# Maxima of two query tiles in one vector instruction, and the value products in one run, in the first attention of a two-layer transformer kernel

## The reference

```python
c_q = x @ Wq_down
c_kv = x @ Wkv_down
q_c = (c_q @ Wq_up).reshape(b, s, N_HEADS, HEAD_DIM)
q_r = (x @ Wq_rope).reshape(b, s, N_HEADS, ROPE)
k_c = (c_kv @ Wk_up).reshape(b, s, N_HEADS, HEAD_DIM)
v_c = (c_kv @ Wv_up).reshape(b, s, N_HEADS, HEAD_DIM)
k_r = x @ Wk_rope
scores = (jnp.einsum('bqhd,bkhd->bhqk', q_c, k_c) + jnp.einsum('bqhd,bkd->bhqk', q_r, k_r)) / scale
attn = jax.nn.softmax(scores, axis=-1)
out = jnp.einsum('bhqk,bkhd->bqhd', attn, v_c)
```

## Time and profile before

| | |
|---|---|
| median of 3 runs | 2729.01 us (2726.97 to 2730.4) |
| profiled execution, from its first to its last instruction | 2727.7 us |
| granted TensorE clock, mean | 0.976 of full speed |
| first attention's loop, first to last row of line 407 | 62.9 to 1499.9 us |
| busy: TensorE, DVE, ACT | 94%, 58%, 41% of the span |

### The profile page before, as it was taken

One profiled execution on the slowest core, in us unless ns is written; L12 is line 12 of the kernel. 1 busy time (PEld: TensorE's weight loads), 2 busy tenths in 40 slices (PEclk: granted clock), 3 DMA queues, 4 the chain that ended last, 5 costly groups with the idle time before them and its releaser, 6 DMA issues. The chain is left out here.

```text
span 2727.7 us, 38579 instructions
## 1 busy us (share of the span) xinstructions
PE 2571.7 (94%) x12487; PEld 1838.7 (67%) x12487; DVE 1579.8 (58%) x2919; ACT 1129.2 (41%) x1832; POOL 439.7 (16%) x519
## 2 busy tenths in 40 slices
PE   6999999999999999999999759989999999999996
PEld 3666666666666666666666436658778778778774
DVE  5666666666666666666666260137566566566566
ACT  3455555555555555555555230014234234243231
POOL 0101010101010101010100010004343343242320
PEclk8899999999999999999999969989999999999998
DMA  5122121212121212121211240010110110110001
GB/s 190 44 43 49 41 49 41 49 41 49 41 49 41 49 41 49 41 49 41 49 41 41 69 138 0 0 54 24 39 38 0 38 38 0 38 38 0 16 1 51
DMA packets 46693, 116.86 MB, mean 43 GB/s; under 512 B 5313, under 2 KB 22721, under 8 KB 40514
## 3 DMA queue, kind: packets, MB, share of 16 engines
q1 hardware_dynamic: 46658, 116.40, 16.3%
HBM read 71.81 MB, written 10.49 MB: 30 GB/s over the span
## 5 line engine op out<-in xcount | busy, mean ns | idle before, releaser
L407 DVE TENSOR_REDUCE row_max<-ps_max 128x1 f32<-128x512 f32 x1024 | 678.1, 689 | 294.0 <-PE ps_max L472 270.4
L361 ACT ACTIVATE probs<-ps_score 128x1024 f32<-128x1024 f32 x512 | 525.6, 1027 | 123.8 <-PE ps_score L487 92.5
L472 PE MATMUL ps_max<-KX,Q 68*128 68x512 f32 x1024 | 396.3, 418 | 46.0 <-DMA KX<-content_k 41.2
L485 PE MATMUL ps_score<-Q,K 128*128 128x512 f32 x1024 | 409.1, 400 | 0.5 <-ACT probs L361 0.5
L487 PE MATMUL ps_score<-Q,K 97*128 97x512 f32 x1024 | 405.7, 396 | 0.0
L472 PEld LDWEIGHTS ps_max<-KX,Q 68*128 68x128 f32 x1024 | 194.3, 190 | 207.1 <-issue 150.3
L401 DVE TENSOR_TENSOR Q<-ps_x,Q 64x512 fp32r<-64x512 f32 x256 | 176.5, 690 | 240.7 <-ACT Q L356 238.9
L356 ACT ACTIVATE Q<-ps_x 64x512 fp32r<-64x512 f32 x256 | 151.9, 593 | 365.3 <-PE ps_x L457 363.8
L497 PE MATMUL ps_o<-probs,V_slot 128*32 128x512 f32 x2048 | 245.8, 598 | 1.1 <-ACT probs L361 1.1
L485 PEld LDWEIGHTS ps_score<-Q,K 128*128 128x128 f32 x1024 | 194.2, 190 | 54.9 <-ACT probs L361 12.1
L487 PEld LDWEIGHTS ps_score<-Q,K 97*128 97x128 f32 x1024 | 194.8, 190 | 41.0
(11 more groups left out here) (217 smaller groups left out, 3952.8 us busy)
## 6 DMA issues: line engine op xcount, KB each, us to landing
Q<-Q SPq DMA_DIRECT2D x64, 512.0 KB, 4.3
w_raw<-in_w_qrope SPq DMA_DIRECT2D x32, 512.0 KB, 3.7
wq_raw<-in_wq SPq DMA_DIRECT2D x8, 1024.0 KB, 5.6
wo_raw<-in_wo SPq DMA_DIRECT2D x8, 1024.0 KB, 4.9
w_raw<-in_w SPq DMA_DIRECT2D x6, 704.0 KB, 4.1
Q<-content_q SPq DMA_DIRECT2D x64, 64.0 KB
K<-content_k SPq DMA_DIRECT2D x64, 64.0 KB
wkv_raw<-in_wkv SPq DMA_DIRECT2D x8, 512.0 KB, 3.5
```

Source lines behind the costliest of these rows:

```text
L361: act.activation(probs[:, j, 2 * half:2 * half + 2, :], ps_score[half][:, :, :], ACT.Exp, scale=SCALE).then_inc(exped, 1)
L407: dve.tensor_reduce(row_max[:, t, j:j + 1], ps_max[t % 2][:, :], axis=AXX, op=ALU.max)\
L472: pe.matmul(ps_max[t % 2][:, :], Q2[0:KC0, b, j, t * P:(t + 1) * P], KX[0:KC0, b, j, :], start=True, stop=True).then_inc(max_made, 1)
L485: pe.matmul(ps_score[half][:, k, :], K1[:, b, t * P:(t + 1) * P], Q1[:, b, j, :], start=True, stop=False)
```

## The change

The two single banks for maxima become one double bank `ps_max` of 128 x 2 x 512. The matmuls of two query tiles (2 half and 2 half + 1) are issued together into its two banks, and one DVE instruction reduces both, over the innermost axis, into two columns of `row_max`. So a step has 8 entries `m` instead of 16. A pair waits until the reduction of the pair before it is done. In `ORDER` all four value products come first, ahead of the first maximum, and the eight pairs are spread over the rest. The turned maxima go to the first bank of the pair.

```diff
-        ps_max = [own.enter_context(nc.psum_tensor(f"ps_max{i}", [P, S], F32)) for i in range(2)]
+        ps_max = own.enter_context(nc.psum_tensor("ps_max", [P, 2, S], F32))
...
-            "v00 v10 m00 v20 v30 m01 q00 m02 q10 m03 m10 q20 m11 s00 l00 m12 s01 m13 "
-            "s10 o00 m20 s11 m21 s20 m22 m23 s21 m30 s30 m31 m32 s31 m33").split()]
+            "v00 v10 v20 v30 m00 q00 m01 q10 m10 q20 m11 s00 l00 s01 "
+            "s10 o00 m20 s11 m21 s20 m30 s21 s30 m31 s31").split()]
...
-            def take_max(n, j, t):
-                dve.wait_ge(max_made, 16 * n + 4 * j + t + 1)
-                dve.tensor_reduce(row_max[:, t, j:j + 1], ps_max[t % 2][:, :], axis=AXX, op=ALU.max)\
+            def take_max(n, j, half):
+                dve.wait_ge(max_made, 8 * n + 2 * j + half + 1)
+                dve.tensor_reduce(row_max[:, 2 * half:2 * half + 2, j], ps_max[:, :, :], axis=AXX, op=ALU.max)\
                    .then_inc(max_taken, 1)
...
-            def max_scores(g, b, n, j, t, wait_free=True):
-
-                if j % 2 == 0 and t == 0:
+            def max_scores(g, b, n, j, half, wait_free=True):
+
+                if j % 2 == 0 and half == 0:
                     pe.wait_ge(q_high, 2 * n + j // 2 + 1)
-                if j == 0 and t == 0:
+                if j == 0 and half == 0:
                     pe.wait_ge(content_in[b], 80 * (g + 1))
                     if wait_free:
                         pe.wait_ge(row_made, n)
                 if wait_free:
-                    pe.wait_ge(max_taken, 16 * n + 4 * j + t - 1)
-                pe.matmul(ps_max[t % 2][:, :], Q2[0:KC0, b, j, t * P:(t + 1) * P], KX[0:KC0, b, j, :],
-                          start=True, stop=True).then_inc(max_made, 1)
+                    pe.wait_ge(max_taken, 8 * n + 2 * j + half)
+                for k in range(2):
+                    t = 2 * half + k
+                    last = pe.matmul(ps_max[:, k, :], Q2[0:KC0, b, j, t * P:(t + 1) * P], KX[0:KC0, b, j, :],
+                                     start=True, stop=True)
+                last.then_inc(max_made, 1)
...
-                    pe.wait_ge(max_taken, 16 * (n + 1))
+                    pe.wait_ge(max_taken, 8 * (n + 1))
```

More of the change, by code:

```diff
@@ L383, in body @@
                         act.wait_ge(row_in, 16 * n)
-                    act.activation(mrow[0:GH, :], ps_max[0][0:GH, :], ACT.Copy, scale=-1.0).then_inc(row_made, 1)
+                    act.activation(mrow[0:GH, :], ps_max[0:GH, 0, :], ACT.Copy, scale=-1.0).then_inc(row_made, 1)
                     if not (first and b == 0):
@@ L427, in _ @@
                 for j in range(2 * pair, 2 * pair + 2):
-                    for t in range(ST):
-                        take_max(0, j, t)
+                    for half in range(2):
+                        take_max(0, j, half)
             def body(g, first, last):
@@ L513, in _ @@
             for j in range(GH):
-                for t in range(ST):
-                    max_scores(0, 0, 0, j, t, wait_free=4 * j + t >= 2)
+                for half in range(2):
+                    max_scores(0, 0, 0, j, half, wait_free=j + half > 0)
             def body(g, first, last):
@@ L528, in body @@
                             queries(g + b, 1 - b, 0, third)
-                    pe.wait_ge(max_taken, 16 * (n + 1))
+                    pe.wait_ge(max_taken, 8 * (n + 1))
                     for t in range(ST):
-                        ins = pe.transpose(ps_max[0][0:GH, t * P:(t + 1) * P], row_max[:, t, :], ident[:, :])
+                        ins = pe.transpose(ps_max[0:GH, 0, t * P:(t + 1) * P], row_max[:, t, :], ident[:, :])
                     ins.then_inc(max_turned, 1)
```

## The result

The changed kernel took 2935.09 us (median of 4 runs, 2927.59 to 2938.82) against 2727.99 us for the kernel before in the same session: ratio 1.0755, 95% interval 1.0735 to 1.0774. It is 7.5% slower. The profiled execution is the fastest of the four (2927.59 us); its span is 2925.8 us, 198.1 us more than before.

The account below looks back on a forecast made before the run. TensorE, busy 94%, bounds the kernel; 4.10 us lost minus 1.07 gained is +3.03 a step. 2727.7 + 188 (62 steps) + 4 (first step) + 7 (before the loop) = 2926.7 profiled, forecast 2928 us, range 2880 to 2990.

Parts of the forecast that it names:

- The reduction, D: One DVE reduction over two banks takes 1.22 us; bounds 0.69 and 1.38 us, the upper being exactly two single reductions.
- The cycle: Reduction to reduction of maximum pairs: release 0.06, load to second matmul 0.34, hand-over 0.43, reduction 1.22; sum 2.05 us.
- The two gains: On TensorE each step: wait for KX gone, 0.75 us; value products run together, 0.32 us; together 1.07 us.
- The idle load time: TensorE's maximum weight loads idle for DVE some five times a step, 0.6 to 1.1 us, about 220 us in all.
- m21 behind the normalisation: After o00, DVE normalises before reducing m20, so m21's second matmul starts at 3.18 instead of 2.08 us: 1.10 lost.
- s10: Score pair needing the exponential of s00; its weight load sits idle 0.61 us, of which 0.44 us a step is lost.
- The slow clock: Rival, 7%: new gaps withdraw TensorE's full clock; m00 to m11 at 1.2 GHz costs 146 us more, 3074 us.
- The row at 2028 us: Profile row of the kernel before: TensorE busy 2.41 of 4 us, clock kept at 1.00; cited against the slow-clock rival.
- Before the loop and the first step: Eight maximum pairs before the loop cost +7 us; step n = 0, without value products and on a slow clock, +4.
- DVE's busy time: In the whole kernel DVE's busy time falls by about 80 us, 1.3 us a step, covered by nothing it could shorten.
- the cheap reduction: Rival, 4%: a double-bank reduction costs only 0.69 us; +0.38 us a step, 2757 us.
- the forecast's own case: The main mechanism, 86%: TensorE waits for double-bank reductions in the loop, net +3.03 us a step, 2928 us.

Follow-up runs that it names:

- half reduction: Changed kernel, but DVE reads only the first 256 columns of either bank, 512 elements per reduction: 2749.81 us, ratio 1.0062 to the kernel before.
- values-first kernel: Kernel before with only v20 and v30 moved ahead of m00, two single banks and 16 maxima kept: 2661.12 us, ratio 0.9739.
- spread order: Changed kernel with another order list, nearly every pair having at least 1.7 us of other matmuls behind it: 2728.64 us, ratio 0.9992 to the kernel before.

## Why the prediction was right

The forecast was 2928 us, the measured median 2935, in the range of 2880 to 2990. The mechanism is right, and so is its size in the loop: 3.03 us a step forecast, 2.99 in the undisturbed steps. That the profiled span (2925.8) lies within 1 us of the forecast for it (2926.7) is luck: the loop took 7 us more than forecast, the start 3 less, and what follows the loop 4.6 less, which nobody forecast. By its steps:

- *The reduction, D.* Taken as 1.22 us from the slope of line 1268, measured 1.226. The Trainium skill's estimate of 1.19 us ("VectorE: DVE Perf Modes", section on the TRN2 errata) is too low by 3%. The upper bound of 1.38 us was too high: two reductions in a row took 1.29.
- *The cycle.* 2.05 us forecast, 2.04 to 2.05 in the rows. The half reduction shows that D enters one for one, in five places.
- *The two gains.* 1.07 us forecast; the kernel that has only them gained 1.07 us a step.
- *The idle load time.* About 220 us forecast in all, 297 measured. The forecast listed the lost time; a waiting load is idle 0.82 us where 0.64 are lost, and 1.30 for m21 where 1.13 are. No term of the sum hangs on it.
- *m21 behind the normalisation.* The forecast put the second matmul 3.18 us after the transposes; the rows have it 1028.10 + 0.34 - 1025.23 = 3.21 us after. Moving m20 ahead of it took 0.92 us away, where the expectation had about 0.8.
- *s10.* Idle load 0.61 forecast, 0.62 measured.
- *The step.* 25.6 us forecast, 25.62 measured in the undisturbed ones.
- *The slow clock.* Held to be a rival with 7%, and priced as if whole stretches of each step ran slowly. The prediction named a clock that drops in the loop as a sign of being wrong, and expected 1.00 from 101 us on; this one step failed. The clock fell in 6 of 62 steps, in another place than was named (behind the waits of m21 and m30, not between m00 and m11), and cost 9 us where the rival had 146. This is the term the sum left out, and it covers the 7 us that the profiled execution's loop had more than forecast (195.1 for 188). The Trainium skill ("TensorE: Matmul & The Clock Gate", on PSUM-queue depth-cycling) warns that such short idles make the clock swing. The trace agrees so far as that with idles of 0.4 to 0.9 us between groups of matmuls the clock did fall, in 6 of 62 steps; in the other 56 the same idles left it at 1.00. The row at 2028 us in the earlier trace rows, which I held against it, does not exclude it.
- *Before the loop and the first step.* 7 and 4 forecast, 5.2 and 2.4 measured: too much by 3 us. The first pairs there still ran 2.05 us apart at full clock, the later ones 2.54 to 2.64. TensorE's timeline of the changed kernel, two pairs of either kind:

```profile
64.59 0.73 PE L474 MATMUL ps_max<-KX,Q 68*128 68x512 f32 x2 [1.32 <-DVE row_max L407]
66.64 0.73 PE L474 MATMUL ps_max<-KX,Q 68*128 68x512 f32 x2 [1.32 <-DVE row_max L407]
...
76.46 1.22 PE L474 MATMUL ps_max<-KX,Q 68*128 68x512 f32 x2 [1.32 <-DVE row_max L407]
79.00 1.22 PE L474 MATMUL ps_max<-KX,Q 68*128 68x512 f32 x2 [1.32 <-DVE row_max L407]
```

- *DVE's busy time* was to fall by about 80 us and fell by 50.5. The 80 were made from mean durations, 16 x 0.689 - 8 x 1.22 = 1.26 us a step. But 1024 x 0.689 is 706 us, and the group is busy for 678.1: reductions in a row overlap, and busy time counts the overlap once. 678.1 - 627.8 is 50.3. The slip touched no term of the sum.
- *The chances.* The slow clock, the cheap reduction and the forecast's own case are 97 in 100 together, and all of them are slower; "slower 0.96" does not add up with them.

What stays open: the four runs of the changed kernel spread by 11 us, those of the values-first kernel by 2. A different number of slow stretches in each run would do that (each costs 1.5 us), and the mean granted clocks on record go with it: 0.975 for the run of 2927.59 us, 0.973 for 2932.13, 0.972 for 2938.05, 0.971 for 2938.82. An estimate from them: 0.004 of 2936 us is 12 us of clock lost, about 10 to 12 us of time, and the runs differ by 11. Only one execution has a profile, so the stretches themselves can't be counted. Nor is it settled what exactly makes the clock fall in one step and not in the next; the runs show only that shorter waits (m20 ahead of o00, half reductions) had none and longer ones had more.

## What to carry to other kernels

Merging two instructions on an engine that is not the bound saves next to nothing where other work covers them (4 us over the loop in the spread order); what counts is whether the bottleneck engine keeps a second buffer to go on with. Where it has none, the other engine's duration stands in its path: there two reductions in place of one cost 61 us, 20 directly and the rest through the clock. A single buffer costs hand-over plus consumer (here 0.82 + 1.23 us) minus the work that stands between two uses, so count that work at each place of the order before you give up the second bank. And take a change of two parts apart: moving the value products together with the banks left alone gave 2661 us, 2.6% under the kernel before, while the whole change lost 7.5%. Look too at which wait stands behind the one that is removed: with the pairs spread, an equal time hid a wait that had gone and one that had come.

## What the runs showed of the hardware that was not expected

- TensorE's granted clock dropped to its lower level in a loop that keeps the engine busy 90% of the time, at a cost of about 1.5 us each time. In the changed kernel it followed a stretch with 2.13 us busy of 3, in 6 of 62 steps and always at the same place of the step, while other steps with the same stretch kept the full clock; with waits longer by 0.065 us at five places it happened in 27 of 62 steps, in 7 of them for twice the loss. In the changed kernel matmuls of 512 columns started 0.43 us apart each time instead of 0.235.
- Two DVE reductions of 512 from PSUM in a row took 1.29 us where one alone takes 0.69, and one of 1024 took 1.226: merging saves 0.06 us, not a whole start-up.
- A waiting pair lost less than its idle load suggests: 0.82 us of idle weight load went with 0.64 us of lost time, since the waiting load is followed by the second matmul after 0.34 us instead of 0.47, and a gap of 0.04 us is normal.
